# A graph layer's edge counts: the zeroing of the table moved from eight ScalarE writes to one DMA, and the one-hots made further ahead

## The reference, cut to what matters

```python
u = x @ root + bias
for r in range(8):
    mask = (edge_type == r).astype(x.dtype)
    sums = segment_sum(msgs * mask[:, None], dst, num_segments=n)   # msgs = x[src]
    cnt = segment_sum(mask, dst, num_segments=n)
    u = u + (sums / maximum(cnt, 1.0)[:, None]) @ weight[r]
```

## Time and profile before

| what | us |
|---|---|
| median of 3 runs | 1857.23 (1856.05 to 1858.44) |
| the profiled execution: device time | 1856.47 |
| its span, first to last instruction | 1854.8 |
| TensorE busy in it | 1758.7 (95%) |
| VectorE busy | 999.0 (54%) |
| ScalarE busy | 491.1 (26%) |
| GpSimd busy | 711.3 (38%) |

### The profile page before, as it was taken

How to read it: one execution, slowest core, us unless ns; L and a number is a source line. 1 busy time by engine, 2 the same in 40 slices (tenths; PEclk the granted TensorE clock), 3 DMA queues, 4 the chain that set the end, 5 groups by cost and what they waited for, 6 DMA issues and landing times.

```text
span 1854.8 us, 27729 instructions
## 1 busy us (share of the span) xinstructions
PE 1758.7 (95%) x9548; PEld 1440.6 (78%) x9548; DVE 999.0 (54%) x2478; ACT 491.1 (26%) x935; POOL 711.3 (38%) x613
## 2 busy tenths in 40 slices
PE   5999999999999999999999999855999999999999
PEld 4774688877787877777787877743899888879987
DVE  7997889985435262545435277777622224351311
ACT  3328788861101010111101154352100000111100
POOL 2100000024353536354353553200585552446862
PEclk9999999999999999999999999957999999999999
DMA  4432232233212213121223542110354351113322
GB/s 130 144 99 76 82 100 82 80 93 115 74 57 62 88 46 95 40 84 45 73 57 119 189 118 79 46 47 7 111 174 143 107 157 36 41 52 119 91 74 67
DMA packets 129654, 162.18 MB, mean 87 GB/s; under 512 B 14288, under 2 KB 75868, under 8 KB 129297
## 3 DMA queue, kind: packets, MB, share of 16 engines
q1 hardware_dynamic: 101743, 121.95, 22.2%
q10 hardware_dynamic: 21730, 22.51, 3.9%
q0 software_dynamic: 6080, 16.40, 2.9%
HBM read 135.51 MB, written 25.30 MB: 87 GB/s over the span
## 4 chain that ended last, share of the span: by engine, by line
PE 77%; DVE 12%; ACT 5%; issue 3%; DVEq 2%; DMA 1%; POOL 1%; ACTq 0%; SPq 0%
PE ps L371 20%; PE ps L372 20%; PE ps L373 19%; PE ps L1378 9%; DVE w_lo L322 1%; PE ps L1001 1%; ACT sc_code L921 1%; DVE adj L988 1%; PE ps L1343 1%; ACT counts L973 1%; DVE key_start L872 1%; PE ps L1298 1%; POOL w_lo L280 1%; DMA w_stage<-in_stream 1%; DMA nat<-in_x 1%
## 5 line engine op out<-in xcount | busy, mean ns | idle before, releaser
L371 PE MATMUL ps<-w_hi,xt_hi 128*125 128x512 f32 x1320 | 539.3, 409 | 12.4 <-DVE xt_lo L560 3.5
L260 POOL TENSOR_TENSOR w_hi<-w_stage,zero 128x512 fp32r<-128x512 f32 x258 | 277.8, 1077 | 678.7 <-PE ps L373 653.9
L372 PE MATMUL ps<-w_lo,xt_hi 128*125 128x512 f32 x1320 | 523.2, 396 | 0.0
L373 PE MATMUL ps<-w_hi,xt_lo 128*125 128x512 f32 x1320 | 521.9, 395 | 0.0
L263 POOL TENSOR_TENSOR w_lo<-w_stage,w_hi 128x512 fp32r<-128x512 f32 x258 | 351.1, 1361 | 20.2
L371 PEld LDWEIGHTS ps<-w_hi,xt_hi 128*125 128x125 f32 x1320 | 246.9, 187 | 71.0 <-DVE xt_lo L560 4.3
L373 PEld LDWEIGHTS ps<-w_hi,xt_lo 128*125 128x125 f32 x1320 | 246.1, 186 | 63.3
L372 PEld LDWEIGHTS ps<-w_lo,xt_hi 128*125 128x125 f32 x1320 | 246.6, 187 | 53.4
L371 PE MATMUL ps<-xt_hi,w_hi 128*128 128x314 f32 x736 | 241.0, 327 | 0.8 <-DVE ring L2584 0.7
L373 PE MATMUL ps<-xt_hi,w_lo 128*128 128x314 f32 x736 | 225.8, 307 | 0.0
L372 PE MATMUL ps<-xt_lo,w_hi 128*128 128x314 f32 x736 | 225.7, 307 | 0.0
(11 more groups left out here) (433 smaller groups left out, 2208.7 us busy)
## 6 DMA issues: line engine op xcount, KB each, us to landing
w_stage<-in_stream SPq DMA_DIRECT2D x374, 256.0 KB, 2.7
pre<-ring POOLq DMA_DIRECT2D x30, 250.0 KB, 4.2
a_qt<-pre_t SPq DMA_DIRECT2D x18, 312.5 KB, 3.8
a_qt<-pre_t ACTq DMA_DIRECT2D x14, 312.5 KB
pre_t<-ring_t POOLq DMA_DIRECT2D x12, 312.5 KB, 3.1
pre_t<-ring_t ACTq DMA_DIRECT2D x12, 312.5 KB
a_vx<-pre SPq DMA_DIRECT2D x9, 312.5 KB
nat<-pre SPq DMA_DIRECT2D x2, 1250.0 KB
```

The lines of the kernel that those rows point to most:

```text
L260: POOL.tensor_tensor(w_hi[:, q, :], w_stage[:, q % NST, :], zero[:].to_broadcast([128, 512]), ALU.add).then_inc(S("hi_done"), 1)
L371: PE.matmul(dst, l_hi, r_hi, start=first, stop=False)
L372: PE.matmul(dst, l_hi, r_lo, start=False, stop=False)
L373: return PE.matmul(dst, l_lo, r_hi, start=False, stop=last)
```

## The change

The table is zeroed by one DMA, which ScalarE issues ahead of scatter step 0: it first writes a tile `zeros` of 125 x 659 floats, and the DMA copies it 19 times into each partition. VectorE waits for its landing (`ld_bt` at 32) where it waited for `mk_zero`. The eight ScalarE writes are gone. The one-hots are made 12 chunks ahead in 16 column buffers (now in the room of the scatter's buffers) and 4 row buffers. Of the first twelve, four chunks' come before the evacuation of group 5 and the rest behind it. In the loop of a pair one of the two one-hots stands between the pair's two adds, except where ScalarE makes the second: there the first comes after both adds. TensorE leaves out a wait on VectorE for the chunks that ScalarE makes.

```diff
--- before.py
+++ after.py
@@ -706,8 +706,13 @@
     assert r_hot + sc_per * 1248 <= R_NAT + T * D * 4
     slot_col = tmp("slot_col", [128, NCHUNK], F32, 1)
     slot_row = tmp("slot_row", [128, NCHUNK], F16, 1)
-    hot_col = [tmp(f"hot_col{i}", [128, SPLIT], F16, 1) for i in range(8)]
-    hot_row = [tmp(f"hot_row{i}", [128, 128, 4], F16, 1) for i in range(2)]
+    NHOT, NROWS = 16, 4
+    hot_col = [at(f"hot_col{i}", [128, SPLIT], F16, r_hot + i * 640) for i in range(NHOT)]
+    assert NHOT * 640 <= sc_per * 1248
+    hot_row = [tmp(f"hot_row{i}", [128, 128, 4], F16, 1) for i in range(NROWS)]
+    ZERO, ZERO_RUN = NBUCKET * NB // 2 + 1, 659
+    assert ZERO % ZERO_RUN == 0
+    zeros = tmp("zeros", [P, ZERO_RUN], F32, 1)
     zero16 = tmp("zero16", [P, NCHUNK], BF16, 1)
     col_off = [tmp(f"col_off{i}", [128, SPLIT], F16, 1) for i in range(2)]
     slot_bits = tmp("slot_bits", [128, 2, NCHUNK], I32, 1)
@@ -936,33 +941,34 @@
         return sig(DVE.drain(), "dve_step")
 
 
-    LEAD_HOT, STARTS = 6, 4
+    LEAD_HOT, STARTS = 12, 4
 
     def pair_bank(g):
         return 4 if g % 2 else 6
 
+    def hist_row(c):
+
+        if c >= 4 * NROWS:
+            DVE.wait_ge(S("hi_pe"), c - 4 * (NROWS - 1))
+        DVE.tensor_tensor(hot_row[c // 4 % NROWS][:], iota_by4[:],
+                          slot_row[:, c:c + 4].unsqueeze(1).to_broadcast([128, 128, 4]),
+                          ALU.is_equal)
+
     def hist_hot(c):
 
-        if c % 4 == 0:
-            if c >= 8:
-                DVE.wait_ge(S("hi_pe"), c - 4)
-            DVE.tensor_tensor(hot_row[c // 4 % 2][:], iota_by4[:],
-                              slot_row[:, c:c + 4].unsqueeze(1).to_broadcast([128, 128, 4]), ALU.is_equal)
-        if c % 6 == 5:
-            return
-        if c >= 8:
-            DVE.wait_ge(S("hi_pe"), c - 7)
-        DVE.tensor_scalar(hot_col[c % 8][:], col_key[:], slot_col[:, bass.ds(c, 1)], None,
+        if c >= NHOT:
+            DVE.wait_ge(S("hi_pe"), c - NHOT + 1)
+        DVE.tensor_scalar(hot_col[c % NHOT][:], col_key[:], slot_col[:, bass.ds(c, 1)], None,
                           ALU.is_equal).then_inc(S("hi_dve"), 1)
 
     def hist_hot_act(c):
 
-        if c >= 8:
-            ALE.wait_ge(S("hi_pe"), c - 7)
+        if c >= NHOT:
+            ALE.wait_ge(S("hi_pe"), c - NHOT + 1)
         off = col_off[c // 6 % 2]
         ALE.activation(off[:], col_key[:], ACT.Abs, scale=-1.0, bias=slot_col[:, c:c + 1]).then_inc(S("hi_act"), 1)
         ALE.wait_ge(S("hi_act"), c // 6 * 2 + 1)
-        ALE.activation(hot_col[c % 8][:], off[:], ACT.Relu, scale=-1.0, bias=ones[:, 0:1]).then_inc(S("hi_act"), 1)
+        ALE.activation(hot_col[c % NHOT][:], off[:], ACT.Relu, scale=-1.0, bias=ones[:, 0:1]).then_inc(S("hi_act"), 1)
 
     def hist_copy(g):
 
@@ -997,8 +1003,9 @@
             c = 2 * g + j
             if c % 6 == 5:
                 PE.wait_ge(S("hi_act"), c // 6 * 2 + 2)
-            PE.wait_ge(S("hi_dve"), c + 1 - (c + 1) // 6)
-            PE.matmul(ps[0:P, pair_bank(g) + j, 0:SPLIT], hot_row[c // 4 % 2][:, 0:P, c % 4], hot_col[c % 8][:],
+            if c % 6 != 5:
+                PE.wait_ge(S("hi_dve"), c + 1 - (c + 1) // 6)
+            PE.matmul(ps[0:P, pair_bank(g) + j, 0:SPLIT], hot_row[c // 4 % NROWS][:, 0:P, c % 4], hot_col[c % NHOT][:],
                       start=True, stop=True).then_inc(S("hi_pe"), 1)
 
     SC0, LEAD = 4, 4
@@ -1041,8 +1048,10 @@
 
         assert C_HAND == SC0 * KT and SC0 == G_PLAIN
         SC_STEPS = -(-EC // sc_per)
-        ZERO = NBUCKET * NB // 2 + 1
-        zero_per = -(-ZERO // KT)
+        wait(ALE, sig(ALE.activation(zeros[:], zero[0:P, :].to_broadcast([P, ZERO_RUN]), ACT.Copy), "act_step"))
+        wait(ALE, mk_ranked)
+        ALE.dma_start(adj[:].bitcast(F32).rearrange("p (n w) -> p n w", w=ZERO_RUN),
+                      zeros[:].unsqueeze(1).to_broadcast([P, ZERO // ZERO_RUN, ZERO_RUN])).then_inc(S("ld_bt"), 16)
 
         def columns(s):
             return [(s * sc_per + j, j) for j in range(sc_per) if s * sc_per + j < EC]
@@ -1076,13 +1085,6 @@
             if s == 0:
                 evacuate_plain(SC0 - 1)
                 load_bias(SC0)
-                wait(ALE, mk_ranked)
-            if 1 <= s <= KT:
-                z0 = (s - 1) * zero_per
-                zn = min(zero_per, ZERO - z0)
-                t_ = ALE.activation(adj[:].bitcast(F32)[:, z0:z0 + zn], zero[0:P, :].to_broadcast([P, zn]), ACT.Copy)
-                if s == KT:
-                    mk_zero = sig(t_, "act_step")
             if s == KT + 1:
                 load_bias(SC0 + 1)
         for s in range(SC_STEPS, SC_GROUPS * KT):
@@ -1097,12 +1099,19 @@
                 evacuate(SC0)
         for s in range(SC_STEPS, SC_GROUPS * KT):
             split_dve(chunk_beside(s))
-        wait(DVE, mk_zero)
+        DVE.wait_ge(S("ld_bt"), 32)
         DVE.wait_ge(S("sc_pe"), sc_per + EC + 1)
         mk_slots = slot_keys()
-        for c in range(LEAD_HOT):
+        for c in range(4):
+            if c == 0:
+                hist_row(c)
             hist_hot(c)
         evacuate(SC0 + 1)
+        for c in range(4, LEAD_HOT):
+            if c % 4 == 0:
+                hist_row(c)
+            if c % 6 != 5:
+                hist_hot(c)
 
         HI0 = SC0 + SC_GROUPS
         assert HI0 + HI_GROUPS == G_PRE0
@@ -1140,9 +1149,10 @@
 
         for h in range(HI_GROUPS):
             dense(h + HI0, hist_step(h))
-        ALE.wait_ge(S("ld_bt"), 16)
+        ALE.wait_ge(S("ld_bt"), 32)
         wait(ALE, mk_slots)
-        hist_hot_act(5)
+        for c in range(5, LEAD_HOT, 6):
+            hist_hot_act(c)
         for h in range(HI_GROUPS):
             for n in range(per):
                 ahead = 2 * (h * per + n) + 1 + LEAD_HOT
@@ -1163,14 +1173,21 @@
         starts = dict(enumerate(hist_starts(0)))
         for h in range(HI_GROUPS):
             for n in range(per):
-                for c in (2 * (h * per + n), 2 * (h * per + n) + 1):
-                    hist_add(c, starts[c])
-                    if c + LEAD_HOT < NCHUNK:
-                        hist_hot(c + LEAD_HOT)
-                    if c % STARTS == 0 and c + STARTS < NCHUNK:
-                        starts.update(zip(range(c + STARTS, c + 2 * STARTS), hist_starts(c + STARTS)))
-                    if c % 2 == 0 and chunk_at(h, n):
-                        split_dve(chunk_at(h, n))
+                c = 2 * (h * per + n)
+                ahead = c + LEAD_HOT
+                by_act = ahead % 6 == 4
+                hist_add(c, starts[c])
+                if ahead % 4 == 0 and ahead < NCHUNK:
+                    hist_row(ahead)
+                if ahead < NCHUNK and not by_act:
+                    hist_hot(ahead)
+                if c % STARTS == 0 and c + STARTS < NCHUNK:
+                    starts.update(zip(range(c + STARTS, c + 2 * STARTS), hist_starts(c + STARTS)))
+                if chunk_at(h, n):
+                    split_dve(chunk_at(h, n))
+                hist_add(c + 1, starts[c + 1])
+                if ahead < NCHUNK:
+                    hist_hot(ahead if by_act else ahead + 1)
 
     dense_to_pre(G_PRE0, B_PRE0, beside)
 
@@ -2586,7 +2603,7 @@
     def evac_turned(g, b):
 
         if (g, b) == (1, 0):
-            DVE.wait_ge(S("ld_bt"), 32)
+            DVE.wait_ge(S("ld_bt"), 48)
         if g - 1 not in TURNED1:
             for m in (b, b + 1):
                 DVE.wait_ge(S(f"stl1_{m}"), 16 * g + 16)
```

## The result

The kernel after takes 1890.58 us (median of 4 runs, 1887.58 to 1890.88), the kernel before 1856.64 (4 runs, 1855.05 to 1858.44): ratio 1.0179 [1.0161, 1.0197]. It is slower by 34 us. I forecast 1878 with a range up to 1884: the sign and the mechanism came out, the size didn't. The profiled execution took 1890.88 us, 34.4 more than the one before.

The account below looks back on a forecast made before the run. TensorE carries 77% of the chain, fed by ScalarE in the scatter, with VectorE fullest in the histogram. 1856.5 - 8.6 (writes) + 35 (hold) + 2 (clock) - 7 (histogram) = 1877.9, given as 1878 us; range 1839 to 1884.

Parts of the forecast that it names:

- Writes removed: Scatter: without ScalarE's zeroing writes, steps 1 to 7 each become 1.23 us shorter, the eighth gives nothing; -8.6 us.
- The issue itself is hidden: Before the scatter: ScalarE is free from 128.4 to near 137, so writing zeros and issuing the DMA cost nothing.
- The DMA uses five engines: Zeroing copy: expected on five of 16 engines, 475 pieces each, 49 us at 128 GB/s.
- The hold of ScalarE: Scatter: group 4's bias issue waits behind the copy until about 180, stalling ScalarE, TensorE and VectorE; +35 us, bounds 0 to 41.
- The release: Bias issue behind the copy: released with an eighth still open, 60 of 475 pieces per engine, after 415 moved.
- my rival without the histogram's gain: Histogram: gives nothing back because VectorE waits for ScalarE's copies instead; 1885 us, no separate chance.
- The clock: TensorE after its long pause: a lowered granted clock loses 1.7 to 5 us; taken as +2.
- The histogram: Histogram: closer VectorE adds -7.4, later first add +0.9, fewer copy waits -0.5; sum -7 us, bounds 0 to -13.
- Other waits: Evacuations, chunk loads and VectorE's wait for the zeroing: the bias row and copy land in time, no added cost.
- The quick copy: Zeroing copy: spreads over 16 engines or doesn't hold ScalarE, so nothing is late; 1841 us, chance 26%.
- The late bias row: Group 4's evacuation: ScalarE isn't held, but the row lands behind the copy, +2 us; 1852 us, chance 12%.
- Half the hold: Scatter: ScalarE is held half as long if pieces move faster within SBUF; 1856 to 1864 us, chance 5%.

Follow-up runs that it names:

- src_hbm: Kernel after, but the row of zeros is first stored to HBM and the 19 copies read it from there: 1876.43 us, ratio 1.0104.
- hist_lead12_old: hist_alone with the old loop order (add, one-hot, add, one-hot), keeping the lead of twelve chunks: 1851.04 us, ratio 0.997.
- hist_alone: Kernel after with the old zeroing by eight ScalarE writes, so only the new histogram is changed: 1845.54 us, ratio 0.9945.
- bias_ahead: Kernel after with both bias rows, the second in its own buffer, issued before the unchanged copy: 1837.15 us, ratio 0.9894.
- pieces_10: Kernel after with the copy in 10 pieces of 5008 bytes per partition instead of 19 of 2636: 1880.03 us, ratio 1.0119.

## Why the prediction was right and where it failed

- **Writes removed, -8.6: right.** Steps of 4.87 us replace those of 6.09. The shift of the first turned matmul, 43.8, is 197.34 - 144.97 = 52.4 of later resumption, less 8.6.
- **The issue itself is hidden: right.** 1.47 us at 128.96, and ScalarE's next work starts at 137.34. The DMA uses five engines: right.
- **The hold of ScalarE, +35: this step failed, by its size.** It measured 52.4 us. The order behind it held (TensorE 54 us and VectorE 55 us for the same issue). What failed is the rate: I took 128 GB/s from the earlier trace rows, loads from HBM, and the copy made 86 GB/s undisturbed and 80 over all. The 402 pieces on each of five engines that had moved at the release are 5.3 MB. They took 65.8 us, from 131.5 to 197.3; at 86 GB/s they are 61.6 us, at 128 GB/s 41.4. So of the 17 us that were missing the rate accounts for 20, and my other factors for -3: the start 1.5 us later than 130, 402 pieces where I had 415 (-1.4), 4 us of shared traffic where I had 7. src_hbm, where the rate was 126, had a hold of 37.92 and 1876.43 us. My upper bound, 41 us, came from the same rate and so was none: no row shows a copy within SBUF, and I let it be quicker than the loads (a rival) but not slower. Why the copy was slower is open.
- **The release: near by luck.** I took it that an issue is released when the transfer ahead has all but gone, and carried an eighth of its bytes over as 60 pieces. But 93 of the second load's 125 per engine were still left at 431.06, where an eighth of the pair is 31, and 73 were left here.
- **The range.** With my own bounds (hold 41, clock 5, histogram 0) the sum is 1893.9, and my rival without the histogram's gain stood at 1885. I closed the range at 1884 all the same.
- **The clock, +2: about nothing.** The granted clock was at 0.50 (1.2 GHz) during the pause and in the mean 0.84 in the ten us behind it. But the steps were 4.87 us from the first on: TensorE had room in a step that ScalarE sets. The earlier trace rows showed the clock, not a loss.
- **The histogram, -7: right in kind, -9.3 measured.** From first to last add 165.3 became 155.3, -10.0, where I had -7.4 and -0.5 of waits; the first add came 1.0 later relative to the first turned matmul (0.9 taken), and TensorE took the cast up 0.3 sooner. The step that was too small is the order: the one-hot between the adds gave 3.8 us (hist_lead12_old) where my distances have 2.0. Such a one-hot fills the time in which the second add of a pair waited, for the first or for ScalarE's copy; the adds' wait for copies went from 5.8 to 0.5 us, and I had counted 0.5 of it as gained. hist_lead12_old and hist_alone, which differ in this order only, bear it out: 4.6 us fewer such waits, 3.8 us less time.
- **Other waits: right.** None of the evacuations waited for a bias row, and VectorE did not wait for the copy's landing at 209.9.
- **The rivals.** The quick copy (1841) did not happen with 125 partitions, and happened with 128 (1838.98). The late bias row falls: ScalarE was held, and in bias_ahead the copy cost the steps beside it nothing (first turned matmul at 224.02). Half the hold falls.

With the measured sizes the sum is 1856.5 - 8.6 + 52.4 + 0 - 9.3 = 1891.0, against 1890.88.

## What to carry to other kernels

A DMA that is "hidden" still stands in its queue: before a large one goes on an engine's queue, look for the next DMA of that same queue and for what the issuing engine computes behind it, and issue the small, needed transfers first. Count how many engines a transfer will get from its partitions, and give it 128 where the room is there; either edit took away some 52 us here. A rate read from a load is not a bound for a copy within SBUF, so the range has to stay open on that side. And what is open at a release is to be counted in pieces per engine, as the engines' records show it.

## What the runs showed of the hardware that I had not expected

- **An issue waits until only some pieces per engine of the transfer ahead on its queue are left**, counted in pieces and not in bytes: 73 of 2636 bytes in the kernel after, 73 of 5008 in pieces_10. The number is not a constant: the holds seen here end with 61 to 115 left. Other queues on the same engines are not held (SyncE 0.33 to 0.39 us). The Trainium skill (DMA: Bandwidth & Descriptors, Issuing engines are not separate DMA queues) calls the time to initiate a DMA usually small; of the bias row it was 52.58 us for a transfer of 250 KB.
- **A long copy within SBUF ran at 80 to 86 GB/s on five engines, short ones at 113 to 123**, and the long one from HBM at 126. The same long copy with the bias rows issued ahead of it needed 118 ns for a piece instead of 150. The cause isn't settled.
- **125 partitions take five engines and 128 take sixteen**: 80 GB/s against 221 for the same copy.
